# A float32 attention layer on one core: tile 0's exponentials written into the DMA-summed buffer, a slot for tile 13 alone, v loaded in pairs of heads

## The reference, cut to what matters

```python
# x: (4, 2048, 512), 16 heads of 32
xn = _layernorm(x)
q = _split_heads(xn @ q_w.T + q_b, 16) / sqrt(32)
k = _split_heads(xn @ k_w.T + k_b, 16)
v = _split_heads(xn @ v_w.T + v_b, 16)
attn = softmax(einsum('bhqd,bhkd->bhqk', q, k))      # 64 (batch, head) pairs, 2048 x 2048 each
ctx = einsum('bhqk,bhkd->bhqd', attn, v)
y = tanh(xn @ weight @ aux_weight1 @ aux_weight2 + bias)
return x + ctx_merged @ out_w.T + out_b + y
```

## Time and profile before

| | us |
|---|---|
| median of 3 runs | 4345.02 (4344.81 to 4345.11) |
| the profiled execution | 4344.67 |
| its span | 4342.9 |
| busy PE / DVE / ACT / POOL in the span | 4196.0 / 2940.9 / 2373.2 / 3186.2 |
| bytes moved by DMA | 740.43 MB, of which 335.56 MB by the joins |

### The profile page before, as it was taken

One profiled execution on the slowest core, in us unless ns is written; L12 is line 12 of the kernel. 1 busy time (PEld: TensorE's weight loads), 2 busy tenths in 40 slices (PEclk: granted clock), 3 DMA queues, 4 the chain that ended last, 5 costly groups with the idle time before them and its releaser, 6 DMA issues.

```text
span 4342.9 us, 77789 instructions
## 1 busy us (share of the span) xinstructions
PE 4196.0 (97%) x21728; PEld 2525.9 (58%) x21728; DVE 2940.9 (68%) x4928; ACT 2373.2 (55%) x4517; POOL 3186.2 (73%) x1119
## 2 busy tenths in 40 slices
PE   7999999899999999999999999999999999999999
PEld 5888888555555555555555555555555555555467
DVE  4343343587777777777777777777777777777433
ACT  1222222066666666666666666666666666666621
POOL 0322322289989999989999999899899999999830
PEclk9999999799999999999999999999999999999999
DMA  4444445367777777777777777777777777777677
GB/s 158 147 166 158 148 168 173 110 152 175 165 169 167 173 170 170 172 179 166 171 167 172 170 173 172 180 166 171 166 169 169 173 171 176 175 165 167 166 236 257
DMA packets 343531, 740.43 MB, mean 170 GB/s; under 512 B 176128, under 2 KB 177152, under 8 KB 281728
## 3 DMA queue, kind: packets, MB, share of 16 engines
q0 software_dynamic: 46080, 335.56, 39.8%
q1 hardware_dynamic: 142912, 220.52, 15.4%
q10 hardware_dynamic: 154176, 179.87, 14.0%
HBM read 195.30 MB, written 137.36 MB: 77 GB/s over the span
## 4 chain that ended last, share of the span: by engine, by line
PE 33%; DMA 23%; POOL 11%; issue 10%; ACT 3%; DVE 1%; POOLq 0%; ACTq 0%; SPq 0%; DVEq 0%
DMA dma_sum<-probs 23%; POOL pool_sum L625 10%; PE pv_bank L851 10%; PE st_bank L845 9%; PE sm_bank L829 9%; ACT probs L680 3%; PE sm_bank L851 2%; PE sm_bank L193 2%; DVE part_max L765 1%; PE st_bank L193 1%; DMA q_stack<-s_ctx 0%; POOL dma_sum L637 0%; ACTq L679 0%; PE sm_bank L838 0%; POOLq L621 0%
## 5 line engine op out<-in xcount | busy, mean ns | idle before, releaser
L765 DVE TENSOR_REDUCE part_max<-sm_bank 128x1 f32<-128x512 f32 x4096 | 2502.4, 680 | 683.6 <-PE sm_bank L829 681.7
L680 ACT ACTIVATE probs<-st_bank 128x512 f32<-128x512 f32 x4096 | 2095.0, 615 | 856.2 <-PE st_bank L845 747.2
L625 POOL TENSOR_TENSOR pool_sum<-pool_sum,probs 128x2048 f32<-128x2048 f32 x512 | 2457.1, 4799 | 136.2 <-ACT probs L680 124.8
L845 PE MATMUL st_bank<-q_stack,k_stack 97*128 97x512 f32 x4096 | 1657.3, 406 | 99.5 <-ACT probs L680 97.2
L829 PE MATMUL sm_bank<-k_stack,q_stack 96*128 96x512 f32 x4096 | 1691.9, 417 | 11.4 <-DVEq L743 9.4
L829 PEld LDWEIGHTS sm_bank<-k_stack,q_stack 96*128 96x128 f32 x4096 | 785.8, 192 | 540.0 <-DVE part_max L765 320.0
L851 PE MATMUL pv_bank<-probs,v_head 128*32 128x512 f32 x8192 | 1034.8, 625 | 0.0
L845 PEld LDWEIGHTS st_bank<-q_stack,k_stack 97*128 97x128 f32 x4096 | 778.9, 190 | 408.2 <-ACT probs L680 256.7
L851 PEld LDWEIGHTS pv_bank<-probs,v_head 128*32 128x32 f32 x8192 | 220.2, 112 | 496.5 <-issue 249.2
L637 POOL DMA_DIRECT2D dma_sum<-probs x320 | 297.5, 930 | 145.7 <-DMA dma_sum<-probs 135.5
L302 POOL TENSOR_TENSOR y_out<-y_out,x_in 128x512 f32<-128x512 f32 x64 | 82.6, 1291 | 370.8 <-ACT y_out L331 364.8
(11 more groups left out here) (85 smaller groups left out, 2048.0 us busy)
## 6 DMA issues: line engine op xcount, KB each, us to landing
dma_sum<-probs POOLq DMA_DIRECT2D x320, 1024.0 KB, 8.3
dma_sum<-probs ACTq DMA_DIRECT2D x64, 1024.0 KB, 6.2
q_stack<-s_q_hi ACTq DMA_DIRECT2D x122, 256.0 KB, 5.3
k_stack<-s_k_hi ACTq DMA_DIRECT2D x122, 256.0 KB, 5.6
x_in<-in_x SPq DMA_DIRECT2D x16, 1024.0 KB, 7.8
s_q_hi<-qk_hi SPq DMA_DIRECT2D x16, 1024.0 KB, 4.3
s_q_lo<-qk_lo SPq DMA_DIRECT2D x16, 1024.0 KB, 6.4
s_k_hi<-qk_hi SPq DMA_DIRECT2D x16, 1024.0 KB, 4.3
```

The lines of the kernel that those rows point to most:

```text
L625: nc.gpsimd.tensor_tensor(total[:], one[:], probs[kt % PROBS][:], ALU.add).then_inc(pool_added, 1)
L680: nc.scalar.activation(probs[kt % PROBS][:, q * BLK:(q + 1) * BLK], st_bank[:, st_place(kt * QB + q)], ACT.Exp, scale=SCALE).then_inc(prob ...
L765: nc.vector.tensor_reduce(part_max[:, k:k + 1], sm_bank[:, sm_place(k)], AX.X, ALU.max).then_inc(max_scores_read, 1)
L845: nc.tensor.matmul(st_bank[:, st_place(u)], k_st[r][0:ROWS + 1, kt * P:(kt + 1) * P], q_st[r][0:ROWS + 1, q * BLK:(q + 1) * BLK], start=Tr ...
```

## The change

Tile 0 no longer has a slot: its exponentials go straight into `dma_sum`, where the joins add the others, PE uses it from there, and the copying DMA (64 of them, 1 MB each) is gone. Join 1 now waits until PE has used tile 0. Slots are given by a table: tiles 1 to 12, 14 and 15 take seven slots in turn, tile 13 has the eighth to itself. The tile that was in a slot before is now:

| tile | 1 | 2 | 3 | 4 | 5 | 6 | 7 | 8 | 9 | 10 | 11 | 12 | 13 | 14 | 15 |
|---|---|---|---|---|---|---|---|---|---|---|---|---|---|---|---|
| before the change | 9' | 10' | 11' | 12' | 13' | 14' | 15' | 0 | 1 | 2 | 3 | 4 | 5 | 6 | 7 |
| after it | 8' | 9' | 10' | 11' | 12' | 14' | 15' | 1 | 2 | 3 | 4 | 5 | 13' | 6 | 7 |

(' means of the head before.) v of two heads (64 numbers, 256 bytes in a row) comes with one DMA, behind tile 15 of every second head, into two buffers with semaphores of their own.

```diff
-PROBS = 8
+CHAINS = [[0, 2, 5, 8, 10, 13]]
+SLOT = {kt: i % 7 for i, kt in enumerate([*range(1, 13), 14, 15])} | {13: 7}
...
+def tile_before(kt):
+    same = [t for t in SLOT if SLOT[t] == SLOT[kt]]
+    i = same.index(kt)
+    return same[i - 1], int(i == 0)
...
+def load_v(eng, dram, h, v_pair, loaded):
+    v_rows = dram["v"][bass.ds((h // HEADS) * SEQ, SEQ), bass.ds((h % HEADS) * DH, 2 * DH)]
+    eng.dma_start(v_pair[:], v_rows.rearrange("(t p) d -> p t d", p=P)).then_inc(loaded, DMA)
...
+        def tile_at(r, kt):
+            starts = [tiles[0] for tiles in CHAINS]
+            return dma_sum[starts.index(kt)][r % 2] if kt in starts else probs[SLOT[kt]]
...
                 if j == 1:
-                    pool.wait_ge(first_copied, PRIME + h * DMA + DMA)
-                    if not (isinstance(h, int) and h == 0):
-                        pool.wait_ge(joined, h * JOINED)
-                else:
-                    pool.wait_ge(joined, h * JOINED + (j - 1) * DMA)
+                    pool.wait_ge(tile_used, PRIME + h * KT + CHAINS[c][0] + 1)
+                if j > 1 or not (isinstance(h, int) and h == 0):
+                    pool.wait_ge(joined[c], h * JOINED[c] + (j - 1) * DMA)
...
-                    if q == 0:
-                        act.wait_ge(tile_used, PRIME + h * KT + kt - PROBS + 1)
-                        old, back = ((kt - PROBS), 0) if kt >= PROBS else (kt - PROBS + KT, 1)
+                    if q == 0 and kt in SLOT:
+                        old, back = tile_before(kt)
+                        act.wait_ge(tile_used, PRIME + h * KT - back * KT + old + 1)
...
-            def first_tile(h, r):
-                act.wait_ge(probs_ready, PRIME + h * UNITS + QB * (DMA_TILES[0] + 1))
-                act.dma_start(dma_sum[r % 2][:], probs[DMA_TILES[0] % PROBS][:]).then_inc(first_copied, DMA)
...
-                load_part(act, dram, h, i, q_st[r], k_st[r], v_sb[r], head_loaded[r])
+                if i < len(PARTS):
+                    load_part(act, dram, h, i, q_st[r], k_st[r], head_loaded[r])
+                elif r % 2:
+                    load_v(act, dram, h - 1, v_sb[r // 2], v_loaded[r // 2])
...
                 if kt == 0:
                     pe.wait_ge(pv_copied, PRIME + h)
+                    if r % 2 == 0:
+                        pe.wait_ge(v_loaded[r // 2], PRIME + (h // GROUP) * DMA + DMA)
```

More of the change, by code:

```diff
@@ L43 @@
 LOAD_AT = [6, 7, 9, 10, 12, 13, 15]
-DMA_TILES = [0, 2, 5, 8, 10, 13]
-POOL_TILES = [kt for kt in range(KT) if kt not in DMA_TILES]
+CHAINS = [[0, 2, 5, 8, 10, 13]]
+POOL_TILES = [kt for kt in range(KT) if not any(kt in tiles for tiles in CHAINS)]
 POOL_ADDS = len(POOL_TILES) - 1
-JOINED = (len(DMA_TILES) - 1) * DMA
-JOIN_AFTER = {0: 1, 2: 2, 4: 3, 6: 4, 7: 5}
+JOINED = [(len(tiles) - 1) * DMA for tiles in CHAINS]
+JOIN_AFTER = {0: (0, 1), 2: (0, 2), 4: (0, 3), 6: (0, 4), 7: (0, 5)}
+SLOT = {kt: i % 7 for i, kt in enumerate([*range(1, 13), 14, 15])} | {13: 7}
 SCALE_ADD = 7
@@ L194, in three_passes, with load_part, load_head @@
     return last
[L197 to L204, removed]
-    else:
-        stack, row = (q_stack if i < 3 else k_stack), (i % 3) * DH
-        eng.dma_start(stack[row:row + DH, :].bitcast(F32), dram[PARTS[i]][bass.ds(h * DH, DH), :]).then_inc(loaded, DMA)
-def load_head(eng, dram, h, q_stack, k_stack, v_head, loaded):
+PARTS = ("q_hi", "q_lo", "q_hi", "k_hi", "k_hi", "k_lo")
+def load_part(eng, dram, h, i, q_stack, k_stack, loaded):
+    stack, row = (q_stack if i < 3 else k_stack), (i % 3) * DH
+    eng.dma_start(stack[row:row + DH, :].bitcast(F32), dram[PARTS[i]][bass.ds(h * DH, DH), :]).then_inc(loaded, DMA)
+def load_v(eng, dram, h, v_pair, loaded):
+    v_rows = dram["v"][bass.ds((h // HEADS) * SEQ, SEQ), bass.ds((h % HEADS) * DH, 2 * DH)]
+    eng.dma_start(v_pair[:], v_rows.rearrange("(t p) d -> p t d", p=P)).then_inc(loaded, DMA)
+def load_head(eng, dram, h, q_stack, k_stack, loaded):
     for i in range(len(PARTS)):
-        load_part(eng, dram, h, i, q_stack, k_stack, v_head, loaded)
+        load_part(eng, dram, h, i, q_stack, k_stack, loaded)
 def build_project(nc, x, dram, keep, first):
@@ L281, in _ @@
             sp.wait_ge(v_stored, PRIME + DMA * TB)
-            load_head(sp, dram, 0, first["q_stack"], first["k_stack"], first["v_head"], first["loaded"])
+            load_head(sp, dram, 0, first["q_stack"], first["k_stack"], first["loaded"])
+            load_v(sp, dram, 0, first["v_pair"], first["v_loaded"])
             for par in range(2):
@@ L452, in build_attend @@
         k_st = [first["k_stack"]] + [sb(f"k_stack{r}", [P, SEQ], F32R) for r in range(1, GROUP)]
-        v_sb = [first["v_head"]] + [sb(f"v_head{r}", [P, KT, DH]) for r in range(1, GROUP)]
-        probs = [sb(f"probs{s}", [P, SEQ]) for s in range(PROBS)]
+        v_sb = [first["v_pair"], sb("v_pair1", [P, KT, 2 * DH])]
+        probs = [sb(f"probs{s}", [P, SEQ]) for s in range(max(SLOT.values()) + 1)]
         pool_sum = [sb(f"pool_sum{s}", [P, SEQ]) for s in range(2)]
-        dma_sum = [sb(f"dma_sum{s}", [P, SEQ]) for s in range(2)]
+        dma_sum = [[sb(f"dma_sum{c}_{s}", [P, SEQ]) for s in range(2)] for c in range(len(CHAINS))]
         ones, ident = sb("ones_att", [P, DH]), sb("ident_att", [P, P])
@@ L469, in build_attend @@
         head_loaded = [first["loaded"]] + [sem(f"head_loaded{r}") for r in range(1, GROUP)]
+        v_loaded = [first["v_loaded"], sem("v_loaded1")]
         row_loaded = [sem(f"row_loaded{r}") for r in range(GROUP)]
@@ L648, in sum_up @@
                 if i in JOIN_AFTER:
-                    join(h, r, JOIN_AFTER[i])
+                    join(h, r, *JOIN_AFTER[i])
             for i in range(POOL_ADDS):
@@ L664, in _, with exps @@
         def _(act):
-            for s in (probs_ready, pv_copied, sums_copied, first_copied):
+            for s in (probs_ready, pv_copied, sums_copied):
                 act.sem_inc(s, PRIME)
-            def exps(h, kt):
+            def exps(h, r, kt):
                 for q in range(QB):
-                    if q == 0:
-                        act.wait_ge(tile_used, PRIME + h * KT + kt - PROBS + 1)
-                        old, back = ((kt - PROBS), 0) if kt >= PROBS else (kt - PROBS + KT, 1)
+                    if q == 0 and kt in SLOT:
+                        old, back = tile_before(kt)
+                        act.wait_ge(tile_used, PRIME + h * KT - back * KT + old + 1)
                         if old in POOL_TILES:
                             act.wait_ge(pool_added, PRIME + h * POOL_ADDS - back * POOL_ADDS + adds_after(old))
[L675 to L678, removed]
+                        elif old != kt and not (back and isinstance(h, int) and h == 0):
+                            c = [old in tiles for tiles in CHAINS].index(True)
+                            act.wait_ge(joined[c], h * JOINED[c] - back * JOINED[c] + CHAINS[c].index(old) * DMA)
                     act.wait_ge(scores_ready, h * UNITS + kt * QB + q + 1)
-                    nc.scalar.activation(probs[kt % PROBS][:, q * BLK:(q + 1) * BLK],
+                    nc.scalar.activation(tile_at(r, kt)[:, q * BLK:(q + 1) * BLK],
                                          st_bank[:, st_place(kt * QB + q)], ACT.Exp,
                                          scale=SCALE).then_inc(probs_ready, 1)
-            def first_tile(h, r):
-                act.wait_ge(probs_ready, PRIME + h * UNITS + QB * (DMA_TILES[0] + 1))
-                act.dma_start(dma_sum[r % 2][:], probs[DMA_TILES[0] % PROBS][:]).then_inc(first_copied, DMA)
             def copy_bank(h, r, bank, copies, ready, value, copied):
```

43 lines of the change are left out of this document (20 added, 23 removed).

## The result

| | us |
|---|---|
| before, in the same session | 4344.92 (4343.79 to 4345.11, 4 runs) |
| the changed kernel | 4284.3 (4278.06 to 4286.54, 4 runs) |
| ratio | 0.9859, 95% interval 0.9842 to 0.9876 |
| forecast | 4213, range 4172 to 4278 |

The change makes the kernel faster by 1.4%. The forecast was 3%, and the range ends 6 us short of the median. From the sums' copies on ACT a head now takes 50.37 us in the mean of 56 (1086.84 to 3907.32), against 51.2.

The account below looks back on a forecast made before the run. A ring through join 5 and tile 5 was taken to bound the head at 51.2 us. 51.2 - 49.2 + 0.1 = 2.1 us over 61 heads, 128, plus 4 made 132: 4345 - 132 = 4213 us, range 4172 to 4278.

Parts of the forecast that it names:

- PE's floor: What PE needs per head by itself: eight pitches of 5.80 us plus 1.9 us for `add_up`, 48.3 us.
- The ring through join 5 and tile 5: Tile 6, POOL's addition 2, joins 4 and 5, next head's tile 5, then tile 6 again: makes the head 51.2 us.
- the half clock behind PE's long stall: Behind a 1.80 us stall PE gets the 1.2 GHz level, costing 1.64 us in every second head.
- the rival at PE's floor: Joins land sooner without the copy, POOL waits less and PE leads at 48.3 us per head: 4164 us, chance 14%.
- So the head goes to POOL's round, 49.2 us: POOL no longer waits for tile 6 and leads; the head falls from 51.2 to 49.2 us, PE waiting some 0.8.
- On ACT one issue goes, and ACT is busy 1899.74 of 2866.94 us: nothing: Dropping the copy's issue from ACT's queue was counted as no change in time.
- The stall moves: Late joins hold tile 3, tile 12 or `add_up`; half clock stays in every second head: 4290 us, chance 16%.
- I take 0.1 us per head: Gain from removing the copy's 1 MB DMA beside join 4: 0.1 us per head, ends 0 and 0.8.
- Tile 5 no longer waits for tile 13; tiles 2, 1 and 11 have time: With the new slots, tile 5's stall and tile 2's wait go; tiles 1 and 11 find their slots free.
- Zero for the seven slots: Seven slots in rotation instead of eight add no waits, as at tile 12; upper end 1.2 us per head.
- v in pairs: Half the v loads, same bytes, 256-byte rows: counted 0, ends -0.1 and +0.2 us per head.

Follow-up runs that it names:

- pad48: The changed kernel with 48 increments of an unused semaphore ahead of ACT's first exponential: 4223.06 us, ratio 0.9722.
- rot8: The changed kernel with tiles 1 to 15 in turn in all eight slots, so tile 13 has none of its own: 4301.24 us, ratio 0.9906.
- late1: The changed kernel with join 1 issued behind POOL's addition 1 instead of addition 0: 4461.75 us, ratio 1.0272.
- vsingle: The changed kernel with 48 increments of an unused semaphore on ACT and v loaded per head again: 4212.44 us, ratio 0.9699.
- before_pad253: The kernel before the change with 253 increments of an unused semaphore on ACT, shifting its loop to the unlucky place: 4365.56 us, ratio 1.0066.
- pad8: The changed kernel with 8 increments of an unused semaphore ahead of ACT's first exponential: 4220.25 us, ratio 0.9717.
- rot8_copy: rot8 with 48 increments on ACT and an idle 1 MB DMA per head where the copy stood: 4329.97 us, ratio 0.9969.
- pad48_copy: pad48 with an idle 1 MB DMA per head where the copy stood, tile 13 keeping its slot: 4224.04 us, ratio 0.9723.

## Why the prediction missed

**Where the engines stand: right but for PE's floor.** The ring through join 5 and tile 5, and the half clock behind PE's long stall, were read correctly. PE's floor was put at 48.3 us per head; it is 48.8. I took one pitch of 5.80 for all eight. The starts of `use` in a head of 48.8 us of the changed kernel have two longer ones, 6.13 (2055.30 to 2061.43) and 6.16 (2084.59 to 2090.75):

```profile
2049.52 1.92 PE L859 MATMUL pv_bank<-probs,v_pair 128*32 128x512 f32 x16
2055.30 1.92 PE L859 MATMUL pv_bank<-probs,v_pair 128*32 128x512 f32 x16
2061.43 1.92 PE L859 MATMUL pv_bank<-probs,v_pair 128*32 128x512 f32 x16
...
2084.59 1.06 PE L859 MATMUL pv_bank<-dma_sum,v_pair 128*32 128x512 f32 x8
...
2090.75 1.92 PE L859 MATMUL pv_bank<-probs,v_pair 128*32 128x512 f32 x16
```

With 48.8 in its sum the rival at PE's floor is 4195 (4345 - 61 x 2.4 - 4), not 4164.

**The step "So the head goes to POOL's round, 49.2 us": right in size once the fetch is out of the way, not in how PE is held.** In pad48 a head takes 49.31 us, POOL waits for a tile's exponentials 1.4 us in all (111.2 before) and for joins 113.7, so POOL has no slack, as said. 4220 to 4223 against the forecast 4213 is within 0.25%. But PE was to wait 0.8 us per head, mostly at tile 3. Its waits in pad48, 1042 to 3850 us:

```profile
PE st_bank L856 <- DMA q_stack<-max_row: 13.1, 24, 1.0
...
PE st_bank L856 <- ACT probs L698: 4.7, 4, 1.3
```

The larger one is for the row of maxima, which the first scores of a new head need. This DMA of 8 KB runs beside joins 3 and 4 and lands in 5.6 us at the median, against 4.9 in the kernel before, and PE stands where it is later than that. ACT's nine waits for joins are four at tile 3 (up to 1.6 us) and five at tile 12 (up to 2.0). How POOL's full round leads to the late row isn't shown.

**The step that failed: "On ACT one issue goes, and ACT is busy 1899.74 of 2866.94 us: nothing".** ACT was priced by its busy time, and the sum had no term for how its program is fetched. In the changed kernel the loop on ACT stands three instructions earlier, and the jump back falls on join 1's traffic. This costs 61 us (4284.3 against 4223.06) of the 71 by which the forecast of 4213 is off: each of the 14 jumps back pays a wait of 3.2 to 4.3 us and then half the clock. The kernel before shows neither sign of it, no wait of ACT for "issue" and 179 packets. It isn't one of the rivals. "The stall moves" gave 4290 and the sign of a half clock that stays, but its mechanism, late joins at tiles 3 and 12, is not what happened: in the changed kernel ACT waits for no join. The time was near by luck.

**The step "I take 0.1 us per head" for the copy: wrong in its cause.** I asked what the copy does to join 4 and found that it meets only its end. It meets join 5, which is the one that tile 5 waited for. The 7.3 us that I read for join 5 beside a copy is one of the short ones; the mean is 8.32. Its traffic is worth 78 us as long as tile 5 waits for that join. With tile 13 in a slot of its own it is worth nothing, so the sum came out right all the same. With the cause put on the slot alone I would have forecast rot8 at 4330 or more; with the pad it is 4252.

**Tile 5 no longer waits for tile 13; tiles 2, 1 and 11 have time: right.** No wait of ACT for a join in the changed kernel, nine in pad48 (tiles 3 and 12). "Zero for the seven slots" nearly holds, 9.9 us at tile 12 in pad48, but the distance is small: 4.5 us on join 1 cost 239 us in late1 (against pad48).

**v in pairs: taken as 0, within -0.1 and +0.2 us per head.** vsingle is faster by 7 to 11 us, 0.1 to 0.2 us per head.

## What to carry to other kernels

When an edit of a tuned loop moves an engine's instructions, look at what that engine does just behind its jump back, and at what is on the DMA queues at that moment. The sign in the profile of the new kernel is a wait for "issue" that recurs once per pass, and one packet more per pass on the instruction queue; the profile before the edit need not show it. If it is there, shift the loop by a few instructions; eight increments of an unused semaphore gave back 64 of 4284 us here. And where two parts of a change loosen the same wait, price them in a table with and without each other: each one alone can look like the whole gain, and their gains don't add.

## What the hardware showed that I had not expected

- ACT's program comes in packets of 8 KB. A loop moved by 8 or 48 instructions fetches 179 packets in the run, at the old place or 128 further on 193 or 194.
- The first such packet behind a jump came 0.5 to 2.1 us after ACT's last work when no join had just started (before_pad253), and 4.0 to 5.1 us after it while a 1 MB accumulating DMA was on the engines (the changed kernel, 91% at one of them). ACT waited for it only with the loop at the unlucky place: in pad8 it was as late (3.0 to 5.3 us) and cost nothing.
- After a stall of PE of 3.06 us the granted clock was 0.50 for over 4 us, and a head with such a stall was 6 us longer than its neighbours, of which the stall itself is half.
- The half clock does not follow from a stall's length alone: in rot8_copy it came behind one of 1.57 us and not behind one of 1.71.
- A plain 1 MB DMA that starts 2 to 6 us ahead of an accumulating one of the same size made it land 1 us later in the mean (7.28 to 8.24 in pad48 and pad48_copy, with the same slots), and by about 2 us in every second head.
